# Two adapter layers in one kernel: another order of the engines' work within a step, and the gathers issued from GpSimd

## The chip, the cores and the metric

One NeuronCore of a Trainium2 chip runs the whole kernel. Its engines are TensorE (PE in the profile), VectorE (DVE), ScalarE (ACT), GpSimd (POOL) and SyncE (SP); each works through its own queue in order, and semaphores hold them together. DMAs are issued from SP's or GpSimd's queue and run on the core's 16 DMA engines. The metric is the time of one execution on the device, in microseconds (us); the time of a kernel is the median of its runs.

## What is computed

x is 64 sequences of 64 tokens with 1024 features, float32. There are two layers, each a LoRA adapter picked by sequence (rank 16), whose output goes through a dense 1024 x 1024 matrix with a bias and a mixture of four experts of rank 8, added to x.

```python
def cond(x, A, B, ids):                     # adapter of each sequence
    Bx = einsum('bni,bri->bnr', x, B[ids])
    return einsum('bnr,bor->bno', Bx, A[ids])

def ffn(c, W, b, EA, EB, RW, bias):         # layer 0: bias = Rb + log(prior)
    gates = softmax(c @ RW.T + bias)        # over 4 experts
    z = einsum('bth,erh->bter', c, EA)
    return c @ W.T + b + 2 * einsum('bter,eor,bte->bto', z, EB, gates)

x = x + ffn(cond(x, A0, B0, id0), W0, b0, ...)
x = x + ffn(cond(x, A1, B1, id1), W1, b1, ...)
```

## The kernel before

**Tiling.** x is kept with features on the partitions. The 64 sequences are cut into 8 steps of 8 sequences (512 tokens). Since the adapters have rank 16, a group of 8 adapters is 128 columns; the kernel never forms the adapters' output in full width but multiplies the adapters' A matrices with the weights (`wide`, 128 x 1060 per step) and then with the tokens' 128 coefficients. Every float32 operand is split into a high and a low part (ScalarE copies the high one, VectorE or GpSimd subtracts to get the low one), and each product is three matmuls (lines 307 to 309): high by high, low by high, high by low.

**A step on each engine** (`body(g, par, last)`; steps 1 to 6 run in a hardware loop on PE, ACT, DVE and POOL, see `steps`):
- SP: reads the 16 adapter ids of step g + 2 into registers (`pick`, L240), waits until step g + 1's adapters are all split (`a_lo`), issues 16 gathers (`gather`, L251 and L253: 64 KB into `b0raw` and 128 KB into `abraw` per sequence), and then stores the four chunks of the step's result from `xraw` (L282), each as soon as VectorE has written it (`d_out`), and loads the chunks of x of step g + 2 into the same buffer (L234), each when its chunk is stored.
- PE: the `ps_h` product (8 rounds over `hr`), `wide(0)`, the transposes of `hsb`, `route(0)`, `wide(1)`, half of `wide(2)`, the `ht` product, `turn()` (transposes `lp`, waits for softmax(0) by `l_done`), the rest of `wide(2)`, `query()` (waits for `htx_ready`, then for `l_lo` and `l_hi`), the first half of the next step's `project`, `route(1)`, the second half of `project`, `turn()`, and then the eight result tiles. A `wide` part has 8 rounds of three matmuls: parts 0 and 2 of 384 columns, part 1 of 292.
- ACT: high parts and PSUM reads in the order of PE's products: `split_b` (four copies into `bst_hi`), `wide_high(0)`, `ht` and `he`, two x copies (`split_x`, wait for the x loads by `x_in`), the exponential of softmax(0) (L686), `wide_high(1)`, `htx`, `coef_high(0)` (`ce_hi`, twice), the other x copies between `wide_high(2)` and the `cf` copies, and so on.
- DVE: low parts, softmax (L869 to L898), and the result tiles (L942: accumulator + bias + x).
- POOL: only the low parts of the first half of x (`xs_lo`, four pieces) and of the adapters' A (`a1s_lo`), L952. It issues DMAs only at the start of the kernel.

`b0raw` and `abraw` are single buffers, so the gather of step g + 2 can't start before step g + 1's adapters have been split. `xraw` is double, `xs` and `bst` are single. The last step holds back the last quarter of `wide(2)` until after the query.

## Time and profile before

| | us |
|---|---|
| median of 3 runs | 334.89 (334.20 to 335.64) |
| the profiled execution | 334.41 |
| its span in the trace | 332.70 |
| PE busy | 307.0 (92% of the span) |
| VectorE, ScalarE, GpSimd busy | 220.1, 186.4, 63.3 |

The span is the time between the first and the last event of the trace; the profiled execution took 1.71 us more than its span. PE's busy time counts overlapping matmuls once, and matmul ends are modelled, so pauses of PE are best read from the idle times that the trace puts ahead of an instruction, and from the distance of starts. The matmul clock granted was 1.00 of 2.4 GHz in the steps, 0.995 on average.

### The profile page before, as it was taken

The numbers are of one execution on the slowest core, as the hardware profiler recorded it, in microseconds if no ns is written. First come the engines' busy times: TensorE is split into PE (matmuls) and PEld (weight loads), VectorE is DVE, ScalarE is ACT, GpSimd is POOL, SyncE is SP. The second block draws the span as 40 slices with busy tenths as digits, with TensorE's granted clock in tenths as the row PEclk, the third lists the DMA queues.
The fourth block names the chain that finished last, engine by engine and source line by source line (L and its number), as shares of the span: only waits on it lengthen the run. The fifth ranks groups of instructions, "written<-read, shape, count | busy, mean of one in ns | idle before, by whom it ended". The sixth has DMA issues, their size and how long they took to land.

```text
span 332.7 us, 6476 instructions
## 1 busy us (share of the span) xinstructions
PE 307.0 (92%) x2048; PEld 284.4 (85%) x2048; DVE 220.1 (66%) x476; ACT 186.4 (56%) x384; POOL 63.3 (19%) x58
## 2 busy tenths in 40 slices
PE   5994998799989998999979999999999999999894
PEld 4453998589978998999979999999999999899783
DVE  2156887686738766686658666777668676864556
ACT  1446976946546565755466465646575657461520
POOL 5600000620042103320143003320332024200000
PEclk9999899999999999999999999999999999999999
DMA  7999973006870388126840587037811783041006
GB/s 267 345 365 381 347 208 156 0 8 167 300 224 0 104 243 302 51 60 212 286 139 0 158 284 250 2 103 244 299 47 55 255 292 92 0 193 62 1 0 252
DMA packets 30773, 56.16 MB, mean 169 GB/s; under 512 B 3633, under 2 KB 20050, under 8 KB 30754
## 3 DMA queue, kind: packets, MB, share of 16 engines
q1 hardware_dynamic: 29666, 52.97, 48.3%
q0 software_dynamic: 1088, 2.97, 2.5%
q8 instruction: 8, 0.13, 0.1%
q14 instruction: 11, 0.09, 0.1%
HBM read 39.15 MB, written 16.78 MB: 168 GB/s over the span
## 4 chain that ended last, share of the span: by engine, by line
issue 41%; PE 20%; DMA 13%; POOL 12%; DVE 6%; ACT 3%; SPq 2%; POOLq 1%; DVEq 0%; ACTq 0%
POOL xs_lo L952 8%; DMA out<-xraw 6%; DMA xraw<-x_in 6%; PE ps_d L307 3%; PE ps_d L309 3%; PE ps_d L308 3%; POOL a1s_lo L952 2%; DVE xs_lo L740 2%; DVE xraw L942 2%; PE ps_d L545 1%; PE ps_p L307 1%; PE ps_d L547 1%; ACT res L574 1%; SPq L253 1%; SPq L251 1%
## 5 line engine op out<-in xcount | busy, mean ns | idle before, releaser
L952 POOL TENSOR_TENSOR xs_lo<-xraw,xs_hi 128x512 fp32r<-128x512 f32 x28 | 36.0, 1290 | 182.5 <-ACT xs_hi L574 182.4
L307 PE MATMUL ps_d<-w1s_hi,a1s_hi 128*128 128x384 f32 (+1 forms) x192 | 63.9, 333 | 0.0
L309 PE MATMUL ps_d<-w1s_hi,a1s_lo 128*128 128x384 f32 (+1 forms) x192 | 62.0, 323 | 0.0
L308 PE MATMUL ps_d<-w1s_lo,a1s_hi 128*128 128x384 f32 (+1 forms) x192 | 61.9, 322 | 0.0
L942 DVE SCALAR_TENSOR_TENSOR xraw<-ps_d,lp,xraw 128x512 f32<-128x512 f32 x60 | 43.6, 748 | 22.5 <-PE ps_d L547 22.5
L574 ACT ACTIVATE xs_hi<-xraw 128x512 fp32r<-128x512 f32 x60 | 36.0, 626 | 26.4 <-DMA xraw<-x_in 25.9
L307 PE MATMUL ps_p<-xs_hi,bst_hi 128*128 128x256 f32 x120 | 36.5, 304 | 6.2 <-DVE bst_lo L740 2.4
L308 PEld LDWEIGHTS ps_d<-w1s_lo,a1s_hi 128*128 128x128 f32 x192 | 36.2, 189 | 0.0
L307 PEld LDWEIGHTS ps_d<-w1s_hi,a1s_hi 128*128 128x128 f32 x192 | 36.1, 188 | 0.0
L309 PEld LDWEIGHTS ps_d<-w1s_hi,a1s_lo 128*128 128x128 f32 x192 | 36.1, 188 | 0.0
L308 PE MATMUL ps_p<-xs_lo,bst_hi 128*128 128x256 f32 x120 | 34.5, 288 | 0.0
L309 PE MATMUL ps_p<-xs_hi,bst_lo 128*128 128x256 f32 x120 | 34.4, 287 | 0.0
L307 PE MATMUL ps_d<-cf,res 128*128 128x256 f32 x120 | 34.4, 286 | 0.0
L309 PE MATMUL ps_d<-cf,res 128*128 128x256 f32 x120 | 33.9, 282 | 0.0
L308 PE MATMUL ps_d<-cf,res 128*128 128x256 f32 x120 | 33.8, 281 | 0.0
L740 DVE TENSOR_TENSOR res<-ps_d,res 64x384 fp32r<-64x384 f32 (+1 forms) x48 | 24.3, 507 | 12.8 <-ACT res L574 12.3
L574 ACT ACTIVATE res<-ps_d 64x384 fp32r<-64x384 f32 (+1 forms) x48 | 21.3, 443 | 18.3 <-PE ps_d L309 17.9
L307 PEld LDWEIGHTS ps_p<-xs_hi,bst_hi 128*128 128x128 f32 x120 | 23.5, 196 | 9.4 <-DVE bst_lo L740 3.3
L952 POOL TENSOR_TENSOR a1s_lo<-abraw,a1s_hi 128x1024 fp32r<-128x1024 f32 x7 | 17.0, 2431 | 39.5 <-ACT a1s_hi L574 39.5
L545 PE MATMUL ps_d<-ce_hi,erows 128*128 128x512 f32 x60 | 24.3, 405 | 0.0
L308 PEld LDWEIGHTS ps_p<-xs_lo,bst_hi 128*128 128x128 f32 x120 | 23.6, 197 | 0.3
L547 PE MATMUL ps_d<-ce_lo,erows 128*128 128x512 f32 x60 | 23.7, 395 | 0.0
(227 smaller groups left out, 702.9 us busy)
## 6 DMA issues: line engine op xcount, KB each, us to landing
out<-xraw SPq DMA_DIRECT2D x31, 512.0 KB, 3.5
xraw<-x_in SPq DMA_DIRECT2D x28, 512.0 KB, 5.0
w_plain<-w SPq DMA_DIRECT2D x16, 512.0 KB, 8.9
abraw<-ab_tab SPq DMA_DIRECT2D x64, 128.0 KB, 2.1
b0raw<-b_tab SPq DMA_DIRECT2D x64, 64.0 KB, 2.0
xraw<-x_in POOLq DMA_DIRECT2D x4, 512.0 KB, 11.0
a_plain<-a SPq DMA_DIRECT2D x1, 512.0 KB, 3.6
out<-xraw SPq DMA_DIRECT2D x2, 256.0 KB, 2.7
```

Of the source, the lines that this page charges most:

```text
L251: sp.dma_start(b0raw[:, b, :], b0_tab[bass.ds(n0, 1)].rearrange("a p n -> p (a n)")).then_inc(signal, 16)
L253: sp.dma_start(abraw[:, b, :, :].rearrange("p a n -> p (a n)"), ab1_tab[bass.ds(n1, 1)].rearrange("a p n -> p (a n)")).then_inc(signal, 16)
L307: pe.matmul(acc, lh, rh, start=first, stop=False, skip_group_check=True)
L308: pe.matmul(acc, lh, rl, start=False, stop=False, skip_group_check=True)
L309: return pe.matmul(acc, ll, rh, start=False, stop=final, skip_group_check=True)
L545: pe.matmul(acc[:], erows[:, m * P:(m + 1) * P], ce_hi[:], start=False, stop=False, skip_group_check=True)
L547: pe.matmul(acc[:], erows[:, m * P:(m + 1) * P], ce_lo[:], start=False, stop=True, skip_group_check=True).then_inc(d_done, 1)
L574: return act.activation(dst, src, ACT.Copy)
L740: return dve.tensor_tensor(dst, whole, high.bitcast(F32), ALU.subtract)
L942: dve.scalar_tensor_tensor(out=xraw[par][:, m, :], in0=banks[m % len(banks)][:], scalar=bsum[:, m:m + 1], in1=xraw[par][:, m, :], op0=ALU. ...
L952: return pool.tensor_tensor(dst, whole, high.bitcast(F32), ALU.subtract)
```

## The change

Nothing is computed differently, and no computing instruction is added or removed; they are put in another order, and 112 gathers (of steps 1 to 7; those of step 0 stay on SP) move from SP's queue to GpSimd's. On SP, `pick` and `gather` leave `body`. On GpSimd, `gather(g + 2)` stands at the end of `body(g)`, behind `split_x` and `split_a`, and reads its 16 ids there, behind the wait on `a_lo`; that of step 1 stands ahead of the steps. GpSimd's loop now runs with its last three steps written out, as SP's did.

```diff
@@ block.sync
-            picks = pick(1)
-            sp.wait_ge(b_lo, 4)
-            sp.wait_ge(a_lo, 1)
-            gather(picks, range(GROUP))
...
-                if ahead:
-                    picks = pick(g + 2)
-                    sp.wait_ge(a_lo, g + 2)
-                    gather(picks, range(GROUP))
@@ block.tensor, body
-                    wide(0)
+                    wide(0, range(3))
...
                 route(0, f0x)
-                if not first:
-                    wide(1)
-                wide(2, range(KT // 2))
+                if first:
+                    wide(2, range(KT // 2))
+                else:
+                    wide(0, range(3, KT))
+                    wide(1, range(2))
                 pe.wait_ge(ht_lo, g + 1)
...
                 turn()
-                wide(2, range(KT // 2, 3 * KT // 4 if last else KT))
+                if first:
+                    wide(2, range(KT // 2, KT))
+                else:
+                    wide(1, range(2, KT))
...
                 query()
-                if last:
-                    wide(2, range(3 * KT // 4, KT))
+                if not first:
+                    wide(2)
...
-                    start_results((0, 1, 2, 3, 4))
+                    start_results((0, 1, 2, 3))
...
-                    from_layers(5)
-                    from_layers(6)
+                    for m in (4, 5, 6):
+                        from_layers(m)
@@ block.scalar, body (whole new order)
+                ht, he copies
+                softmax_exp(0)
+                if not last and not first:
+                    split_b(g + 1)
+                htx copies
+                coef_high(0)
+                wide_high(0)
+                if first:
+                    split_b(g + 1, QUARTERS[0:2])
+                if not last:
+                    split_x(g + 1, 1 - par, 0)
+                wide_high(1)
+                cf copies
+                if first:
+                    m0x_high(0, 2, ps_h)
+                wide_high(2)
+                if first:
+                    split_b(g + 1, QUARTERS[2:4])
+                if not last:
+                    split_x(g + 1, 1 - par, 1)
+                softmax_exp(1)
@@ block.vector, body (whole new order up to softmax(1))
+                c0_low(g); h_to_sbuf(g)
+                softmax(0)          # ht and he lows now inside it, ahead of the wait for exp_done
+                coef_low(0)
+                if not last:
+                    split_b(g + 1, (0, 1) if first else range(4))
+                wide_low(0)
+                the query's four pieces, cf lows
+                wide_low(1)
+                if first:
+                    split_b(g + 1, (2, 3))
+                split_second_x(g + 1, 1 - par, [0, 1, 2])
@@ block.gpsimd
+            def gather(g):
+                n0s, n1s = values(g * GROUP, GROUP, ADAPT0), values(g * GROUP + SEQS, GROUP, SEQS)
+                for b, (n0, n1) in enumerate(zip(n0s, n1s)):
+                    pool.dma_start(b0raw[:, b, :],
+                                   b0_tab[bass.ds(n0, 1)].rearrange("a p n -> p (a n)")).then_inc(gathered, 16)
+                    pool.dma_start(abraw[:, b, :, :].rearrange("p a n -> p (a n)"),
+                                   ab1_tab[bass.ds(n1, 1)].rearrange("a p n -> p (a n)")).then_inc(gathered, 16)
...
             def body(g, par, last):
                 if not last:
                     split_x(g + 1, 1 - par, 0, range(CH))
                     split_a(g + 1)
-
-            steps(pool, body)
+                if not (isinstance(g, int) and g >= STEPS - 2):
+                    pool.wait_ge(a_lo, g + 2)
+                    gather(g + 2)
+
+            pool.wait_ge(b_lo, 4)
+            pool.wait_ge(a_lo, 1)
+            gather(1)
+            steps(pool, body, 3)
```

For ACT and DVE the piece of the diff above tells the new order in short; a line there that isn't code names a group of copies.

**ScalarE, the part of a loop step from the `ht` copy to the softmax's exponential.** `lg<-lg` is the exponential. Before:

```order
L574 ACTIVATE ht<-ps_t 128x128 [waits ht_done]
L574 ACTIVATE he<-ps_t 32x128
L579 REGISTER_ALU
L580 ISA [waits x_in0]
L574 ACTIVATE xs_hi<-xraw 128x512 [waits x_used]
L580 REGISTER_ALU [waits x_in1]
L574 ACTIVATE xs_hi<-xraw 128x512 [waits x_used]
L685 ISA
L686 ACTIVATE lg<-lg 128x16 [waits sm_step]
```

and now, up to the coefficients (`ce_hi`):

```order
L571 ACTIVATE ht<-ps_t 128x128 [waits ht_done]
L571 ACTIVATE he<-ps_t 32x128
L678 ISA
L679 ACTIVATE lg<-lg 128x16 [waits sm_step]
L583 REGISTER_ALU
L571 ACTIVATE bst_hi<-abraw 128x4x8x16 [waits gathered]
L571 ACTIVATE bst_hi<-b0raw 128x4x8x16 x2
L571 ACTIVATE bst_hi<-abraw 128x4x8x16
L571 ACTIVATE htx<-ps_h 64x256 [waits htx_done]
L571 ACTIVATE htx<-ps_h 64x256
L672 ISA
L571 ACTIVATE ce_hi<-ps_t 64x512 [waits t_done]
```

The two x copies with their waits for `x_in` have left the place ahead of the exponential, and the four copies from the gathered buffers, which stood at the step's start, are now between the exponential and `htx`.

**GpSimd, the end of a loop step.** Before:

```order
L952 TENSOR_TENSOR xs_lo<-xraw,xs_hi 128x512 [waits x_hi]
L956 REGISTER_ALU
L952 TENSOR_TENSOR xs_lo<-xraw,xs_hi 128x512 [waits x_hi]
L962 REGISTER_ALU
L952 TENSOR_TENSOR a1s_lo<-abraw,a1s_hi 128x8x8x16 [waits a_hi]
L956 ISA
L952 TENSOR_TENSOR xs_lo<-xraw,xs_hi 128x512 [waits x_hi]
```

and now:

```order
L941 TENSOR_TENSOR xs_lo<-xraw,xs_hi 128x512 [waits x_hi]
L951 REGISTER_ALU
L941 TENSOR_TENSOR a1s_lo<-abraw,a1s_hi 128x8x8x16 [waits a_hi]
L978 ISA [waits a_lo]
L978 TENSOR_LOAD ids
L978 ISA x17
L978 TENSOR_LOAD ids
L978 ISA x16
L985 ISA
L985 DMA b0raw<-b_tab 128x128
L987 ISA
L987 DMA abraw<-ab_tab 128x256
```

Behind `a1s_lo` the next step's first `xs_lo` followed; now two loads of eight ids and 16 DMAs (the last two rows repeat eight times) stand between.

**PE, from the `ht` product of a loop step to the next `wide` rounds.** Before:

```order
L309 MATMUL ps_d<-w1s_hi,a1s_lo 128x384
L478 MATMUL ps_h<-ht,pick 128x128 [waits ht_lo]
L478 MATMUL ps_h<-ht,pick 128x128
L481 REGISTER_ALU
L445 MATMUL ps_t<-ident,lp 128x128 [waits l_done]
L445 MATMUL ps_t<-ident,lp 128x128 x3
L307 MATMUL ps_d<-w1s_hi,a1s_hi 128x384
```

and now:

```order
L301 MATMUL ps_d<-w1s_hi,a1s_lo 128x292
L472 MATMUL ps_h<-ht,pick 128x128 [waits ht_lo]
L472 MATMUL ps_h<-ht,pick 128x128
L475 REGISTER_ALU
L437 MATMUL ps_t<-ident,lp 128x128 [waits l_done]
L437 MATMUL ps_t<-ident,lp 128x128 x3
L299 MATMUL ps_d<-w1s_hi,a1s_hi 128x292
```

The turn has moved forward in the step: it now stands in the middle of part 1 (292 columns) instead of part 2 (384), and all of part 2 comes after the query.

## Rows read from the trace of the kernel before

**Rows 1.** Busy time by stretch, steps 1 to 6; columns are named in the first line.

```profile
core 0: us, PE busy (x) PEld busy (x) DVE busy (x) ACT busy (x) POOL busy (x), PEclk, DMA share, GB/s
...
154.58:191.75 37.17, 35.13 (x248) 33.62 (x247) 24.79 (x56) 21.27 (x46) 7.56 (x5) 1.00 0.51 160
...
262.80:297.82 35.02, 34.81 (x249) 33.59 (x247) 25.37 (x56) 21.28 (x46) 7.62 (x5) 1.00 0.48 167
sum 216.49, PE 209.88 PEld 201.62 DVE 151.03 ACT 127.71 POOL 45.49; mean PE 34.98 PEld 33.60 DVE 25.17 ACT 21.29 POOL 7.58
```

**Rows 2.** The same view, step 0.

```profile
40.37:81.33 40.96, 37.20 (x256) 34.70 (x255) 30.81 (x62) 27.69 (x55) 7.51 (x5) 1.00 0.36 107
```

**Rows 3.** Waits of the whole span: who for whom, us in all, times, longest.

```profile
ACT xs_hi L574 <- DMA xraw<-x_in: 25.9, 18, 2.6
...
PE ps_t L445 <- DVE lp L898: 6.2, 6, 1.7
```

**Rows 4.** Timeline, SP's queue: start, us, instruction.

```profile
155.38 0.96 SPq L282 DMA_DIRECT2D out<-xraw  x2
158.83 0.35 SPq L234 DMA_DIRECT2D xraw<-x_in  x1
```

**Rows 5.** Timeline, ScalarE; in brackets the idle time ahead and its releaser.

```profile
166.92 0.63 ACT L574 ACTIVATE xs_hi<-xraw 128x512 fp32r<-128x512 f32 x1 [2.62 <-DMA xraw<-x_in]
```

**Rows 6.** Timeline, PE, the turn of the same step.

```profile
169.30 0.66 PE L445 MATMUL ps_t<-ident,lp 128*128 128x128 f32 x4 [1.73 <-DVE lp L898]
```

**Rows 7.** Timeline, PE, in the fastest step (from 262.80).

```profile
276.72 0.34 PE L307 MATMUL ps_d<-w1s_hi,a1s_hi 128*128 128x384 f32 x1
277.25 0.34 PE L307 MATMUL ps_d<-w1s_hi,a1s_hi 128*128 128x384 f32 x1
...
279.02 0.40 PE L494 MATMUL ps_s<-ce_hi,he 128*128 128x512 f32 x1
...
285.91 0.39 PE L307 MATMUL ps_p<-xs_hi,bst_hi 128*128 128x256 f32 x1
```

**Rows 8.** Timeline, ScalarE, in the same step.

```profile
265.13 0.63 ACT L574 ACTIVATE bst_hi<-abraw 128x512 fp32r<-128x512 f32 x1 [0.49 <-PE ps_h L316]
...
266.71 0.62 ACT L574 ACTIVATE bst_hi<-abraw 128x512 fp32r<-128x512 f32 x1
...
275.83 0.78 ACT L574 ACTIVATE htx<-ps_h 64x256 fp32r<-64x256 f32 x2 [0.97 <-PE ps_h L478]
...
277.13 0.63 ACT L574 ACTIVATE ce_hi<-ce_hi 64x512 fp32r<-64x512 f32 x1
```

**Rows 9.** Timeline, GpSimd, in step 0 and in step 6.

```profile
58.50 5.08 POOL L952 TENSOR_TENSOR xs_lo<-xraw,xs_hi 128x512 fp32r<-128x512 f32 x4 [44.59 <-ACT xs_hi L574]
...
286.53 2.43 POOL L952 TENSOR_TENSOR a1s_lo<-abraw,a1s_hi 128x1024 fp32r<-128x1024 f32 x1 [5.37 <-ACT a1s_hi L574]
```

**Rows 10.** Line 240, SP's reading of ids: ns min/median/max, first and last start.

```profile
L240 SPq SEQ_ASSERT  x128: 18/18/33, 6.6 to 245.2; - x128
L240 SPq TENSOR_LOAD <-ids x16: 522/527/741, 5.6 to 242.7; - x16
```

**Rows 11.** Tile `exp_plain`, four dynamic DMAs from GpSimd's queue: same columns.

```profile
L971 POOLq MOVE exp_plain<-exp x4: 29/29/29, 3.7 to 5.6; - x4
L971 POOL DMA_DIRECT2D exp_plain<-exp x4: 537/537/547, 4.3 to 6.1; - x4
...
DMA to landing us min/median/max: 5.3/5.5/5.7
```

**Rows 12.** DMA issues: queue, count, KB each, median us from issue to landing.

```profile
abraw<-ab_tab SPq DMA_DIRECT2D x64, 128.0 KB, 2.1
...
ident<-identity POOLq DMA_DIRECT2D x1, 64.0 KB, 3.8
```

**Rows 13.** Timeline, VectorE, the `cf` pieces of step 0 and of step 6.

```profile
62.89 1.41 DVE L740 TENSOR_TENSOR cf<-cm,cf 64x256 fp32r<-64x256 f32 x2 [2.34 <-ACT cf L574]
...
281.65 0.87 DVE L740 TENSOR_TENSOR cf<-cm,cf 64x256 fp32r<-64x256 f32 x2 [0.16 <-ACT cf L574]
```

**Rows 14.** Timeline, PE, route(1) of the last step.

```profile
316.78 0.27 PE L314 MATMUL ps_z<-f1s,cf 128*128 128x72 f32 x1 [2.07 <-DVE cf L740]
```

More of the change, by code:

```diff
@@ L245, in pick, with gather @@
                 return tuple(zip(values(g * GROUP, GROUP, ADAPT0), values(g * GROUP + SEQS, GROUP, SEQS)))
-            def gather(picks, seqs, signal=gathered):
+            def gather(picks, seqs, signal):
                 for b in seqs:
@@ L663, in body @@
                 first = isinstance(g, int) and g == 0
-                if not last and not first:
-                    act.wait_ge(h_done, g + 1)
-                    split_b(g + 1)
                 def wide_high(n):
@@ L686, in softmax_exp @@
                     act.activation(ex[:], lg[:], ACT.Exp).then_inc(exp_done, 1)
-                wide_high(0)
                 act.wait_ge(ht_done, g + 1)
@@ L691, in body @@
                 copy(he[0:LR, :], ps_t[0:LR, P:2 * P]).then_inc(ht_hi, 1)
+                softmax_exp(0)
                 if not last and not first:
-                    split_x(g + 1, 1 - par, 0, [0, 1])
-                softmax_exp(0)
-                wide_high(1)
+                    split_b(g + 1)
                 act.wait_ge(htx_done, g + 1)
@@ L703, in body @@
                 if not last:
-                    split_x(g + 1, 1 - par, 0, range(CH) if first else [2, 3])
-                wide_high(2)
-                if first:
-                    split_b(g + 1, QUARTERS[2:4])
-                if not last:
-                    split_x(g + 1, 1 - par, 1, [0])
+                    split_x(g + 1, 1 - par, 0)
+                wide_high(1)
                 act.wait_ge(c1_done, 2 * g + 1)
@@ L717, in body @@
                     m0x_high(0, 2, ps_h)
+                wide_high(2)
+                if first:
+                    split_b(g + 1, QUARTERS[2:4])
                 if not last:
-                    split_x(g + 1, 1 - par, 1, range(1, CH))
+                    split_x(g + 1, 1 - par, 1)
                 softmax_exp(1)
@@ L845, in body @@
                     h_to_sbuf(g)
-                if not last and not first:
-                    split_b(g + 1)
                 def wide_low(n):
@@ L883, in softmax @@
                                       ALU.subtract).then_inc(sm_step, 1)
+                    if layer == 0:
+                        dve.wait_ge(ht_hi, 2 * g + 2)
+                        low(ht[:, 1, :], ps_t[:, 0:P], ht[:, 0, :])
+                        low(he[ELO, :], ps_t[0:LR, P:2 * P], he[0:LR, :]).then_inc(ht_lo, 1)
                     if layer == 1 and not last:
@@ L900, in softmax @@
                                       .to_broadcast([P, TT, EXP, ER]), ALU.mult).then_inc(l_done, 1)
+                softmax(0)
+                coef_low(0)
+                if not last:
+                    split_b(g + 1, (0, 1) if first else range(4))
                 wide_low(0)
-                dve.wait_ge(ht_hi, 2 * g + 2)
-                low(ht[:, 1, :], ps_t[:, 0:P], ht[:, 0, :])
-                low(he[ELO, :], ps_t[0:LR, P:2 * P], he[0:LR, :]).then_inc(ht_lo, 1)
-                softmax(0)
-                wide_low(1)
-                coef_low(0)
-                if first:
-                    split_b(g + 1, (0, 1))
                 dve.wait_ge(q_done, g + 1)
@@ L985, in _, with values @@
                                ).then_inc(x0_in[i], 16)
+            def values(first, count, limit):
+                return nc.values_load_multi_w_load_instructions(
+                    ids[0:1, bass.ds(first, count)], (mybir.EngineType.Pool,), min_val=0, max_val=limit - 1)[1]
+            def gather(g):
[5 more added lines that the diff above has]
+                                   ab1_tab[bass.ds(n1, 1)].rearrange("a p n -> p (a n)")).then_inc(gathered, 16)
             def body(g, par, last):
```

## The prediction

> **What bounds the kernel now.** I read the stretches by step first, then the list of waits, then single rows. A step here runs from PE's first matmul of one `body` (the `ps_h` product) to that of the next. The six steps 1 to 6 take 216.49 us together, PE is busy for 209.88 of it at granted clock 1.00 (2.4 GHz), and one step takes between 35.0 and 37.2 us [rows 1]; step 0 takes 40.96 us [rows 2]. So the matmuls set the time and little can be won: only PE's pauses. In the list of waits one is large: PE's `turn()` waits six times for `lp`, 6.2 us in all [rows 3]. The cause lies upstream. ScalarE waits 25.9 us in 18 places for `xraw<-x_in` [rows 3], and in a loop step the second of these waits stands ahead of the exponential of softmax(0): it cost 2.62 us at 166.92 [rows 5], and PE's turn, which needs that softmax, waited 1.73 us [rows 6]. The x blocks are late because SP issues 16 gathers first; its first store of the step goes out at 155.38 and its first x load at 158.83 [rows 4], 0.8 us and 4.3 us after the step began at 154.58, though the first result tiles had been finished during the tail of the step before.
>
> **What goes.** (a) SP without gathers stores and loads about 6 us earlier, so ScalarE no longer waits for x. (b) ScalarE also does the exponential before any x copy. (c) On PE, between route(0) and the turn there stand 15 matmuls of 384 columns and 6 of 292 instead of 24 and 12; that is shorter (about 3.4 us), but softmax(0) now has VectorE to itself and needs about 2.7 us. So I cost the turn's wait at nothing; its cover is 0.7 us. The fastest step, 262.80 to 297.82, is the one without that wait, 35.02 us [rows 1]. Two pauses remain in it: one of 0.30 us ahead of the matmul at 285.91 [rows 7] and a like one some 2.5 us earlier, both behind VectorE's late `xs_lo` pieces. With a punctual gather they shrink to nearly nothing, so an unhindered step is 34.6 us, and six are 207.6: **-8.9 us**. (d) In the last step PE waits 2.07 us for `cf` ahead of route(1) [rows 14]; six matmuls were its cover (part 2, the last quarter), and now 24 are, 4.2 us. The wait goes: **-2.2 us** with its restart. (e) Step 0: its turn no longer waits, up to 0.9 us, but Pool's pieces end when they did, so PE only waits later. VectorE, already late there (its two `cf` pieces took 1.41 instead of 0.87 us, since it stood behind Pool's `xs_lo` until 63.58) [rows 9, 13], now has the four lows of part 1 ahead of the `b` and second `x` pieces. Bounds: -0.9 to one Pool piece more, 5.08 / 4 = +1.3 [rows 9]; I take **+1.0**, near the upper end, because PE waits for VectorE at that place now.
>
> **What comes: the gather is late.** Pool's `a1s_lo` ends at 288.96 [rows 9], 8.9 us before the next step begins at 297.82. From here on in step time (0 is that beginning): SP had its ids in registers when this came; Pool reads them after the wait. On SP the last load of eight begins at 242.7 and its last assertion at 245.2 [rows 10]: 2.5 us for eight, 5.0 for 16, and Pool is at -3.9. Then 16 DMAs. Four dynamic ones on Pool had their address moves from 3.7 to 5.6, one per 0.6 us, each starting 0.6 us after its move [rows 11]. So the sixteenth starts at -3.9 + 0.6 + 15 x 0.6 = +5.7. On SP the same sixteen were out at about 0. When do they land? SP's gathers took 2.1 us and Pool's first DMA, with few transfers before it, 3.8 us [rows 12]; Pool's `exp_plain` with all 16 engines busy took 5.3 to 5.7 [rows 11]. Bounds 2.1 and 5.5; I take 3.8, the row nearest to the case: the gather now runs beside the stores and x loads, of which one or two are in flight. **Landing at +9.5.**
>
> Who waits: ScalarE's `split_b`, whose place moved from the step's start to behind the exponential (+6.3: h product 2.0, nine matmuls 1.6, transposes and route(0) 1.3 until VectorE has them, its four pieces 1.1, the exponential 0.3), and everything behind it: `htx`, `ce_hi`, then PE's query. Four copies take 2.2 us (265.13 to 267.33), then from the start of `htx` to the end of the second `ce_hi` it is 1.9 us (275.83 to 277.76) [rows 8], and VectorE's `ce_lo` ends with it: query's second half can start at 9.5 + 2.2 + 2.0 + 0.1 = +13.8. PE reaches it earlier than now: before, at 279.02 - 262.80 = 16.2; without the eight rounds of part 2, 0.53 us each (276.72 to 277.25), at +12.0 [rows 7]. **Wait: 1.8 us per step** (0.1 with SP's landing of 2.1, 3.5 with 5.5). Part 2 behind the query doesn't hide it, since PE works in order.
>
> Second, what followed in time on an engine is now pressed together: VectorE does the four `bst_lo` and two `cf` pieces while Pool does `xs_lo`. In step 0 a `cf` piece stood until Pool was done [rows 9, 13]. Late ScalarE copies put Pool's 5.1 us just ahead of the first half's product and route(1). On time there is 1.3 us of room, late there is none. Bounds 0 and 1.3 us (one Pool piece); I take **0.5**. The Trainium skill says the same, in SBUF — State Buffer, section Who interferes with whom: a DVE instruction with two SBUF inputs contends with a GpSimd one that reads SBUF, the second blocks. By that rule, the trace agrees (1.41 against 0.87 us) [rows 13].
>
> **Sum.** -8.9 - 2.2 + 1.0 = -10.1 us, and 6 x (1.8 + 0.5) = +13.8 us: +3.7. The profiled execution took 334.41 us (its span of 332.70 and 1.71 around it), so 338.1; the median of the runs is 0.48 above it: **338.6 us**. The gather counts six times, since the gathers of steps 2 to 7 are issued at the end of steps 0 to 5; that of step 1 may start at 35.5 us, when `a1s_lo` of step 0 is done, so it lands at about 35.5 + 5.0 + 0.6 + 9.0 + 3.8 = 54, ahead of step 0's first `b` copy (by the rows of before not earlier than 56).
>
> **Rivals.**
> 1. **The gather is on time.** Landing as fast as SP's, 2.1 us, gives +7.8, the wait is 0.1 and Pool's pieces find room: 334.9 - 10.1 + 0.6 = 325 us. For it: one step's traffic is 5.6 MB for 35 us, DMA share 0.48 to 0.51 [rows 1], so the engines aren't full on average. Against it: no DMA of Pool in this trace landed in less than 3.8 us, and stores, loads and gathers now fall in the same 15 us. Chance 0.15. The Trainium skill, DMA: Bandwidth & Descriptors, section on the anatomy of one DMA (SWDGE), gives 2.0 us plus bytes by 436 GB/s, for 128 KB 2.3 us; as an estimate by that page the wait is 0.3 us and the time about 326. The trace doesn't agree where it can be seen (3.8 us for 64 KB).
> 2. **Half late.** Landing after about 3 us: +8.7, wait 1.0, press 0.2: 334.9 - 10.1 + 7.2 = 332 us. Chance 0.13.
> 3. **Even.** After about 3.4 us the wait is 1.4 and the press 0.3, which gives back just what was won: 335 us. Chance 0.15.
> 4. **The forecast**, slower. The tipping point between faster and slower is a loss of 1.7 us per step (10.1 / 6), a landing at about +9.1. Chance 0.42.
> 5. **Much later.** With x loads in all engines Pool's DMAs land after 5 us: wait 3.0, press 0.7, 334.9 - 10.1 + 22.2 = 347 us. Chance 0.15.
>
> **How the numbers follow.** Likeliest is case 4, 338.6 us. The range goes down to 327 and up to 348: case 1 is left out below for the most part (0.13) and the far part of case 5 above (0.06). About 0.5% (1.7 us) is what a measurement of this kernel can tell from no change. Faster: cases 1 and 2, 0.28. Same: 0.15. Slower: 0.57. The likeliest case's own range is 336.6 to 343.
>
> **What would show it.** Right: ScalarE's first `bst_hi` of a loop step has an idle time ahead of it released by the DMA of `abraw` or `b0raw`, some 3 us in steps 1 to 6, and PE idles 1.5 to 2.5 us at `ps_s` (query), no longer at the turn; Pool's first gather DMA starts some 5.6 us after `a1s_lo` ends and the last 9 us later; route(1) of the last step starts without a wait; SP's first store of a step comes some 6 us before the step's begin. Wrong in the sense of case 1: no idle time ahead of `bst_hi` and steps of 34.6 us. What else would break it: ids read faster on Pool than on SP, a pitch of its DMAs below 0.5 us (then everything is 1.5 us earlier and the kernel is faster), or x copies that still wait for DMA because loads and gathers share the engines.

## The result

The changed kernel takes **363.87 us** (median of 4 runs, 361.95 to 365.15); the kernel before, run beside it on the same chip, 335.26 us. The ratio is 1.0856, interval 1.0811 to 1.0901. The prediction was 338.6 us with a range of 327 to 348.

The stretches of the changed kernel by step (same view and columns as [rows 1, 2]; the first row is step 0, then three of the six loop steps with the sum of all six, then the last step):

```profile
core 0: us, PE busy (x) PEld busy (x) DVE busy (x) ACT busy (x) POOL busy (x), PEclk, DMA share, GB/s
40.52:84.48 43.96, 39.65 (x256) 37.50 (x255) 31.41 (x62) 28.11 (x55) 20.03 (x28) 0.92 0.36 117
...
124.78:165.92 41.14, 36.84 (x249) 35.64 (x247) 25.68 (x56) 21.46 (x46) 16.83 (x22) 0.92 0.41 142
...
289.60:330.84 41.24, 36.51 (x249) 34.78 (x247) 25.69 (x56) 21.45 (x46) 14.32 (x17) 0.96 0.38 142
sum 246.36, PE 220.31 PEld 211.74 DVE 154.12 ACT 128.72 POOL 97.25; mean PE 36.72 PEld 35.29 DVE 25.69 ACT 21.45 POOL 16.21
...
330.84:363.40 32.56, 27.70 (x190) 26.37 (x188) 18.71 (x45) 9.43 (x23) 0.00 (x0) 0.96 0.21 84
```

The six loop steps went from 216.49 [rows 1] to 246.36 us, 29.9 more; step 0 from 40.96 [rows 2] to 43.96, 3.0 more; the last step from 34.88 to 32.56, 2.3 less. With 0.15 us at the start that is the 30.7 us between the spans 332.7 and 363.4.

Who waits (columns as [rows 3]). ScalarE no longer waits for x, but for the gather, once in each loop step:

```profile
POOL b0raw L985 <- issue: 62.5, 10, 27.8
...
ACT bst_hi L571 <- DMA abraw<-ab_tab: 38.0, 6, 6.8
...
ACT xs_hi L571 <- DMA xraw<-x_in: 3.0, 3, 1.4
...
PE ps_t L437 <- DVE lp L890: 0.3, 1, 0.3
```

The wait for x, 25.9 us before [rows 3], is down to these 3.0, all of them in the first 25 us, and that of the turn is down from 6.2 to 0.3: in the steps both are gone, as forecast. One round of the new wait follows, from the timelines (start, us, instruction, idle time ahead and its releaser), in order of time. ScalarE, the step from 165.92:

```profile
178.66 0.63 ACT L571 ACTIVATE bst_hi<-abraw 128x512 fp32r<-128x512 f32 x1 [6.54 <-DMA abraw<-ab_tab]
...
180.87 0.78 ACT L571 ACTIVATE htx<-ps_h 64x256 fp32r<-64x256 f32 x2
```

PE in the same step, the last matmul of part 1 and the query that waits for `htx`:

```profile
177.02 0.29 PE L301 MATMUL ps_d<-w1s_hi,a1s_lo 128*128 128x292 f32 x1
181.71 0.58 PE L299 MATMUL ps_s<-cf,htx 128*128 128x256 f32 x1 [4.39 <-ACT htx L571]
```

VectorE, from the coefficients' low part on; up to `lg` at 194.41, which ScalarE's exponential waits for, it has no idle time:

```profile
182.17 0.68 DVE L731 TENSOR_TENSOR ce_lo<-ps_t,ce_hi 64x512 fp32r<-64x512 f32 x1 [8.83 <-ACT ce_hi L571]
```

ScalarE, later in the step:

```profile
194.63 0.22 ACT L679 ACTIVATE lg<-lg 128x16 f32<-128x16 f32 x1 [1.51 <-DVE lg L869]
194.75 1.04 ACT L571 ACTIVATE a1s_hi<-abraw 128x1024 fp32r<-128x1024 f32 x1
```

GpSimd, from there on (14 more DMAs at the same pitch up to the last row):

```profile
195.87 2.43 POOL L941 TENSOR_TENSOR a1s_lo<-abraw,a1s_hi 128x1024 fp32r<-128x1024 f32 x1 [5.53 <-ACT a1s_hi L571]
203.99 0.55 POOL L985 DMA_DIRECT2D b0raw<-b_tab  x1 [5.69 <-issue]
204.59 0.54 POOL L987 DMA_DIRECT2D abraw<-ab_tab  x1
...
212.75 0.54 POOL L987 DMA_DIRECT2D abraw<-ab_tab  x1
```

ScalarE, in the next step:

```profile
220.14 0.63 ACT L571 ACTIVATE bst_hi<-abraw 128x512 fp32r<-128x512 f32 x1 [6.78 <-DMA abraw<-ab_tab]
...
222.35 0.78 ACT L571 ACTIVATE htx<-ps_h 64x256 fp32r<-64x256 f32 x2
```

These rows close a **loop**. From `htx` to `a1s_hi` 13.88 us, to `a1s_lo` 1.12, to the first gather DMA 8.12 (the subtraction's 2.43 and the 5.69 in which GpSimd reads 16 ids), to the sixteenth DMA 8.76 (one per 0.58), to the first copy of what has landed 7.39, to the next `htx` 2.21: together 41.48 us, the distance of the two `htx` (222.35 - 180.87) and the step's length. That the pieces add up to that distance is only arithmetic. What makes them a loop is that each begins when the one before lets it: `htx` stands right behind the copies of B, VectorE works through its row without a gap, `a1s_hi` follows the exponential, `a1s_lo` follows `a1s_hi`, the ids and the DMAs follow `a1s_lo`, and the copies of B wait for the DMAs. No piece waits for PE. So it is not a step of 35 us with a wait on top; the gather calls itself again, and a microsecond taken out of the loop should shorten the step by as much, until something else is longer. The experiments try that.

Of the DMAs the page says (queue, count, KB, median us from issue to landing), beside 2.1 and 2.0 on SP before [rows 12]:

```profile
xraw<-x_in SPq DMA_DIRECT2D x28, 512.0 KB, 6.6
...
abraw<-ab_tab POOLq DMA_DIRECT2D x56, 128.0 KB, 6.5
b0raw<-b_tab POOLq DMA_DIRECT2D x56, 64.0 KB, 6.4
```

The DMA engines are full just then. Over the step from 165.92 their mean share is 0.42, but from the start of its gather's sixteenth DMA (171.51) to the copy (178.66) it is 0.98:

```profile
171.51:178.66 7.15, 5.80 (x42) 5.57 (x40) 1.64 (x8) 0.22 (x1) 0.54 (x1) 1.00 0.98 366
```

After PE's pause the granted clock is at half: 0.50 of 2.4 GHz from 181.7 to 186, and 1.00 again from 187 on; the matmul at 181.71 takes 0.58 us. The stretches show it as 0.92 in the first four loop steps and 0.96 in the last two.

### The profile page after: what moved, and what is told of

Read it like the earlier page. It is cut to its first block, busy times and chain, and to the rows that moved or that the text cites. A ratio compares the mean times of both kernels' runs of the same rounds, so it can differ in the third digit from the quotient of the medians.

```text
span 363.4 us, 6464 instructions
## 1 busy us (share of the span) xinstructions
PE 319.7 (88%) x2048; PEld 297.1 (82%) x2048; DVE 223.5 (62%) x476; ACT 187.8 (52%) x384; POOL 127.6 (35%) x171
## 4 chain that ended last, share of the span: by engine, by line
issue 22%; DVE 19%; PE 17%; DMA 15%; ACT 10%; POOLq 8%; POOL 7%; DVEq 0%; ACTq 0%
DMA abraw<-ab_tab 11%; POOLq L978 6%; DVE bst_lo L731 4%; POOL a1s_lo L941 4%; ACT bst_hi L571 4%; DVE xs_lo L731 4%; DMA xraw<-x_in 3%; PE ps_d L299 3%; PE ps_d L300 3%; PE ps_d L301 3%; DVE res L731 2%; ACT a1s_hi L571 2%; DVE ps_s L904 2%; DVE cm L907 1%; DVE xraw L931 1%
## 5 line engine op out<-in xcount | busy, mean ns | idle before, releaser
L941 POOL TENSOR_TENSOR xs_lo<-xraw,xs_hi 128x512 fp32r<-128x512 f32 x28 | 40.0, 1458 | 81.4 <-ACT xs_hi L571 81.4
L299 PE MATMUL ps_d<-w1s_hi,a1s_hi 128*128 128x384 f32 (+1 forms) x192 | 66.7, 348 | 0.0
L300 PE MATMUL ps_d<-w1s_lo,a1s_hi 128*128 128x384 f32 (+1 forms) x192 | 64.6, 337 | 0.0
L301 PE MATMUL ps_d<-w1s_hi,a1s_lo 128*128 128x384 f32 (+1 forms) x192 | 64.5, 336 | 0.0
L985 POOL DMA_DIRECT2D b0raw<-b_tab x56 | 30.2, 539 | 64.5 <-issue 62.5
L731 DVE TENSOR_TENSOR ce_lo<-ps_t,ce_hi 64x512 fp32r<-64x512 f32 x16 | 10.9, 683 | 61.5 <-ACT ce_hi L571 61.5
L299 PEld LDWEIGHTS ps_d<-w1s_hi,a1s_hi 128*128 128x128 f32 x192 | 38.9, 203 | 0.6
L301 PE MATMUL ps_p<-xs_hi,bst_lo 128*128 128x256 f32 x120 | 35.4, 295 | 0.0
L987 POOL DMA_DIRECT2D abraw<-ab_tab x56 | 30.1, 538 | 3.7 <-issue 1.3
L571 ACT ACTIVATE bst_hi<-abraw 128x512 fp32r<-128x512 f32 x16 | 9.9, 620 | 38.1 <-DMA abraw<-ab_tab 38.0
L299 PE MATMUL ps_s<-cf,htx 128*128 128x256 f32 x16 | 6.4, 402 | 25.2 <-ACT htx L571 25.2
```

What stands on the lines that cost most here:

```text
L299: pe.matmul(acc, lh, rh, start=first, stop=False, skip_group_check=True)
L300: pe.matmul(acc, lh, rl, start=False, stop=False, skip_group_check=True)
L301: return pe.matmul(acc, ll, rh, start=False, stop=final, skip_group_check=True)
L571: return act.activation(dst, src, ACT.Copy)
L731: return dve.tensor_tensor(dst, whole, high.bitcast(F32), ALU.subtract)
L941: return pool.tensor_tensor(dst, whole, high.bitcast(F32), ALU.subtract)
```

## The experiments

Each kernel ran beside the kernel before on the same chip; ratios are against that.

### Which half of the change costs

`e_order`: the new order of all engines, the gathers on SP as before.

```diff
+                if ahead:
+                    picks = pick(g + 2)
+                    sp.wait_ge(a_lo, g + 2)
+                    gather(picks, range(GROUP))
...
-                if not (isinstance(g, int) and g >= STEPS - 2):
-                    pool.wait_ge(a_lo, g + 2)
-                    gather(g + 2)
```

> The new order of PE, ACT and DVE alone; all gathers stay on SP's queue as in the kernel before, ids read ahead of the wait. Theory (the late gather of GpSimd's queue is the loss, and with it the halved clock): ScalarE's first bst_hi of a loop step has no wait for a gather, PE none at ps_s, granted clock 1.00; SP's stores and x loads are late again, but ScalarE now wants x only at about +12 us of a step, so some 1 us of waits is left: steps of 35 to 36 us, 326 to 333 us in all. Rival (the order itself loses, since VectorE and GpSimd are pressed together and ScalarE reads PSUM later): steps of 38 us or more, over 345 us.

Measured: 338.84 us, ratio 1.0142 (1.009 to 1.0193). That lies between my two ranges. The order alone doesn't win 10 us, it loses 4. Its stretches, two of the loop steps with the sum of all six, and step 0:

```profile
157.70:195.52 37.82, 36.27 (x248) 34.99 (x247) 24.06 (x56) 21.35 (x46) 8.10 (x5) 0.95 0.51 159
195.52:231.48 35.96, 34.96 (x249) 33.56 (x247) 24.08 (x56) 21.38 (x46) 8.07 (x5) 1.00 0.50 158
...
sum 218.88, PE 212.41 PEld 204.21 DVE 144.51 ACT 128.22 POOL 48.53; mean PE 35.40 PEld 34.03 DVE 24.09 ACT 21.37 POOL 8.09
```

```profile
40.48:84.42 43.94, 39.66 (x256) 37.51 (x255) 31.37 (x62) 28.05 (x55) 7.61 (x5) 0.92 0.36 108
```

So of the 29.9 us in the loop steps 2.4 are the order's (218.88 - 216.49) and 27.5 the gather's (246.36 - 218.88), 4.6 a step; step 0's 3.0 us are there without the late gather. These are differences of single profiled executions: `before` and `e_last` below have the same code in these six steps, and their sums differ by 1.2 us (216.49 and 215.33), so 2.4 is not much. No step comes near the 34.6 that I had put down: at full clock they take 35.7 to 36.1, two have a stretch of half clock and take some 1.8 more.

`e_queue`: the old order, the gathers on GpSimd.

```diff
-                if ahead:
-                    picks = pick(g + 2)
-                    sp.wait_ge(a_lo, g + 2)
-                    gather(picks, range(GROUP))
...
+                if not (isinstance(g, int) and g >= STEPS - 2):
+                    pool.wait_ge(a_lo, g + 2)
+                    gather(g + 2)
```

> The old order of all engines; only the gathers of steps 1 to 7 are issued from GpSimd's queue, behind split_a, ids read there. Theory: the gather lands at about +12.7 us of a step as in the changed kernel (363.9 us); in the old order split_b stands at the step's start, so ht, the exponential and the turn wait for it too: PE pauses 5 to 6 us per step and the clock falls: 365 to 380 us. Rival (the gather is harmless and the order is the loss): under 340 us.

Measured: 387.93 us, ratio 1.1613 (1.1528 to 1.1698), above what I expected. Its steps take 44.4 to 45.4 us. B is split here ahead of everything else in the step; I take it that the same loop is longer by that, but have not summed it. Its row of the waits:

```profile
ACT bst_hi L566 <- DMA abraw<-ab_tab: 64.9, 6, 11.0
```

So the loss doesn't need the new order: with the old one the late gather costs more (a wait of 64.9 instead of 38.0 us).

### Taking time out of the loop

`e_ids_ahead`: the changed kernel, but GpSimd reads the 16 ids at the start of its body, ahead of its other work.

```diff
             def body(g, par, last):
+                if ahead:
+                    picks = pick(g + 2)
...
                     pool.wait_ge(a_lo, g + 2)
-                    gather(g + 2)
+                    gather(*picks)
```

> The changed kernel, but GpSimd reads the 16 ids of step g + 2 at the start of body(g), ahead of the x pieces, when it has nothing to do, and not behind the wait on a_lo. Theory (serial time on the gather's path, 5.6 us ids and first issue, 8.8 us for 16 issues, 6.6 us landing): it lands 5 us earlier, at about +7.7, PE's pause at ps_s goes or is under 0.5 us, granted clock 1.00, steps of 34.6 to 35.5 us: 325 to 331 us. Rival (the landing is bound by the x traffic on the DMA engines, not by the issue): it lands hardly earlier, over 345 us.

Measured: 337.94 us, ratio 1.0137 (1.0061 to 1.0213): 26 us of the 29 are gone, though not all that I expected. One round of the loop here:

```profile
128.34 0.78 ACT L571 ACTIVATE htx<-ps_h 64x256 fp32r<-64x256 f32 x2
...
146.46 0.55 POOL L988 DMA_DIRECT2D b0raw<-b_tab  x1 [0.67 <-POOL a1s_lo L941]
...
155.27 0.54 POOL L990 DMA_DIRECT2D abraw<-ab_tab  x1
...
162.35 0.63 ACT L571 ACTIVATE bst_hi<-abraw 128x512 fp32r<-128x512 f32 x1 [1.49 <-DMA abraw<-ab_tab]
...
164.57 0.79 ACT L571 ACTIVATE htx<-ps_h 64x256 fp32r<-64x256 f32 x2
```

Behind `a1s_lo` 0.67 us are left of the 5.69, so the reading itself was 5.0 us. From `htx` to the first gather DMA it is now 18.12 us instead of 23.12, to the sixteenth 8.81, to the copy 7.08, to the next `htx` 2.22: 36.23 us. The loop still sets the steps: 5.0 us were taken from it, and the steps fell by 4.4 in the mean, to 36.6 (sum 219.83). Its mark is that ScalarE still waits for the gather once in each loop step, 11.5 us in all. The median landing is 4.8 us.

`e_small_x`: the changed kernel, but in the loop SP stores and loads only the first eighth of each block of x, so most of the result is left out.

```diff
+                    n = TOK if last else TOK // 8
-                                 xraw[par][:, KC * i:KC * (i + 1), :]).then_inc(stored[i], 16)
+                                 xraw[par][:, KC * i:KC * (i + 1), 0:n]).then_inc(stored[i], 16)
```

> The changed kernel with the x loads of steps 2 to 7 and the stores of steps 0 to 6 cut to an eighth of the tokens (64 of 512), so that the DMA engines carry almost only the gathers; the rest of x is old data and most of the output isn't written. Theory (contention with 512 KB transfers makes the 6.6 us from issue to landing): median landing of the gathers falls to 2.3 to 3.8 us, PE's pause at ps_s to 1 to 2 us, 336 to 346 us. Rival (GpSimd's descriptors are slow by themselves): landing stays over 5.5 us and the time over 355 us.

Measured: 338.29 us, ratio 1.0113 (1.0052 to 1.0174). The gathers come from the same queue at the same place; the page's DMA issues (columns as above):

```profile
abraw<-ab_tab POOLq DMA_DIRECT2D x56, 128.0 KB, 2.5
b0raw<-b_tab POOLq DMA_DIRECT2D x56, 64.0 KB, 2.5
```

They land in 2.5 instead of 6.5 us. The 4 us are the traffic of x beside them, not GpSimd's queue. The loop is still there (ScalarE waits for the gather in all six loop steps, 13.0 us), with 2.3 to 2.9 us in place of the 7.39 from the sixteenth DMA to the copy. By the sum above this leaves 36.4 to 37.0 us, and the steps take 36.4 to 37.8 (the 37.8 is one whose sixteen DMAs took 10.0 us instead of 8.8).

`e_fill`: the changed kernel with 19 matmuls of no use where PE pauses.

```diff
+                if not first and not last:
+                    for _ in range(19):
+                        pe.matmul(ps_z[:], erows[:, 0:P], erows[:, 0:TOK], start=True, stop=True,
+                                  skip_group_check=True)
                 query()
```

> The changed kernel with 19 more matmuls of 512 columns ahead of the query of steps 1 to 6. They read weights that are there since the start and write a PSUM bank that nobody reads at that time, so they add about 4.1 us of work that stands where TensorE now waits 3.4 to 4.6 us for the gather; they change nothing of the result. Theory (a part of the loss is the halved clock after the pause, since matmuls of the step run at 0.58 instead of 0.28 us until 4.6 us of work are done): the clock stays at full speed in steps 1 to 6, the pause itself stays as long as the gather is late, and each of the four steps with 0.92 gives back about 2.3 us, each of the two with 0.96 about 1.7 us: 364 - 12.6 = 351 us, between 348 and 355. Rival (the clock costs nothing, since the gather of the next step sets the pace anyway): within 2 us of 364. Second rival (the added matmuls are late work of their own): 366 to 372.

Measured: 365.29 us, ratio 1.0876 (1.0801 to 1.0951), as the changed kernel. The first rival holds, my theory falls. The clock stayed up and the steps stayed long; two of its loop steps, and ScalarE in the first of them:

```profile
166.12:206.71 40.59, 39.77 (x267) 37.24 (x266) 25.68 (x56) 21.37 (x46) 16.79 (x22) 1.00 0.42 141
206.71:247.98 41.27, 40.02 (x268) 37.15 (x266) 25.70 (x56) 21.37 (x46) 16.83 (x22) 1.00 0.41 142
```

```profile
180.41 0.78 ACT L575 ACTIVATE htx<-ps_h 64x256 fp32r<-64x256 f32 x2
...
194.29 1.04 ACT L575 ACTIVATE a1s_hi<-abraw 128x1024 fp32r<-128x1024 f32 x1
```

From `htx` to `a1s_hi` it is again 13.88 us, now with PE at full clock. The half clock costs nothing in the loop: VectorE's row sets that stretch, and it has no gap in either kernel. A busy PE (39.8 of 40.6 us, with matmuls of no use among them) is no sign that it bounds.

### What holds a step of the new order

In `e_order` ScalarE still waits for x (22.9 us, [rows 3] had 25.9), and VectorE for `cf` behind it; its waits:

```profile
ACT xs_hi L579 <- DMA xraw<-x_in: 22.9, 15, 2.4
...
DVE cf L739 <- ACT cf L579: 17.5, 7, 3.9
```

`v_woven`: SP issues half of the gathers, and the rest between the stores and loads of x.

```diff
-                    gather(picks, range(GROUP))
+                    gather(picks, range(0, 4))
...
+                    if ahead and i == 1:
+                        gather(picks, range(4, 6))
+                    if ahead and i == 2:
+                        gather(picks, range(6, 8))
```

> The new order of the engines, all gathers by SyncE's queue, but woven among the stores and loads of x: the first four sequences, store 0, two sequences, store 1 and load 0, the last two sequences, and so on. What tells it from the new order with the gathers in one piece (338.8 us) is that loads of x leave some 2 to 4 us sooner. If late loads of x are what holds that kernel (the copy to xs_hi waits 22.9 us in sum for them, the sum cf behind it comes late, and two steps lose 1.8 us to a halved clock): 334 to 336 us. If the projection is bound by the low parts of x on GpSimd and VectorE whatever the loads do, as the kernel with early ids (36.0 to 36.2 us a step, no wait for x) has it: 337 to 339.

Measured: 335.92 us, ratio 1.0021 (0.9978 to 1.0065), at the edge of the first range. The wait for x falls from 22.9 to 9.7 us, but the loop steps only from 218.88 to 218.51. Where x is on time, the gather is late again: its last DMA leaves SP's queue 3.4 to 4.3 us after the beginning of the step and not at about the beginning, and ScalarE waits 0.9 to 2.2 us for it in the first five loop steps. It doesn't in the sixth, and that one is the shortest of all:

```profile
ACT bst_hi L583 <- DMA abraw<-ab_tab: 8.0, 5, 2.1
...
265.17:300.04 34.87, 34.61 (x248) 33.47 (x247) 25.69 (x56) 21.52 (x46) 8.24 (x5) 1.00 0.41 144
```

Step 0 is 42.81 us here with the clock at 1.00, 1.1 less than in `e_order`, but PE began it 1.8 us sooner (38.72 against 40.48) and came to the turn later in the step. From the turn on like stands against like: 54.23 to 84.42 in `e_order`, 30.19 us, and 53.01 to 81.53 here, 28.52, with the same waits for the low parts of x. So of step 0's 3.0 us the half clock is 1.7, and 1.3 are left for the order.

`v_both`: the same, with step 0 of ScalarE and VectorE in the old order.

```diff
+                if first:
+                    wide_high(0)
                 act.wait_ge(ht_done, g + 1)
...
-                wide_high(0)
+                if not first:
+                    wide_high(0)
```

> The one before it, with step 0 of ScalarE and VectorE back in the old order; steps 1 to 7 keep the new. Step 0 took 43.9 us in the new order and 40.96 in the old; if the order alone does that, this kernel is 3 us under the woven one (331 to 333 if that has 335). If step 0 is long for another reason (the gathers of step 1), within 1 us of it.

Measured: 334.79 us, ratio 1.0013 (0.9973 to 1.0054). Step 0 is 40.95 us again, so the order does it, not the gathers of step 1: ahead of the first b pieces stand the evictions of part 0. The medians differ by 1.1 us, near the 1.3 above and not the 3 that I expected. The loop steps, whose code is the woven kernel's, came out 1.7 us longer in the profiled run (220.20); that much such a sum varies. Their lengths follow the wait for the gather: 35.4 and 35.8 us where it is 0.7 and 0.8, 36.9 to 37.6 where it is 1.9 to 2.8.

What PE waits for in the loop of `v_both` is small and spread: 0.5 us for `f1s`, 0.25 to 0.45 for `xs_lo` of either engine, a few tenths between the projection's matmuls. The timeline of VectorE in `e_ids_ahead`, from the coefficients' low part on:

```profile
129.64 0.68 DVE L731 TENSOR_TENSOR ce_lo<-ps_t,ce_hi 64x512 fp32r<-64x512 f32 x1 [3.57 <-ACT ce_hi L571]
130.25 0.68 DVE L731 TENSOR_TENSOR bst_lo<-abraw,bst_hi 128x512 fp32r<-128x512 f32 x1
...
135.54 2.57 DVE L731 TENSOR_TENSOR cf<-cm,cf 64x256 fp32r<-64x256 f32 x2
138.14 0.19 DVE L731 TENSOR_TENSOR f1s<-ps_d,f1s 64x36 fp32r<-64x36 f32 x1
...
139.26 1.90 DVE L731 TENSOR_TENSOR xs_lo<-xraw,xs_hi 128x512 fp32r<-128x512 f32 x3
```

It stands 3.57 us ahead of `ce_lo` and then works for 13 us without a gap, which makes this row a link of the loop in `e_ids_ahead` and in the changed kernel. The four `bst_lo`, which the old order had at the step's start, and the lows of parts 0 and 1, which it had ahead of `ce_lo`, are now inside, and two `cf` take 2.57 instead of 0.87 us [rows 13] beside GpSimd's `xs_lo`.

`v_both2`: ScalarE copies x ahead of the evictions of part 0, VectorE subtracts part 0 behind `cf`.

```diff
                 else:
+                    wide_high(0)
                     wide_high(1)
...
                 if not first:
+                    wide_low(0)
                     wide_low(1)
```

> The one before it, and in steps 1 to 6 two more moves: ScalarE copies the four chunks of x for GpSimd ahead of its evictions of the first wide product (1.0 us), and VectorE subtracts that product's low part (1.13 us) behind the sum cf instead of ahead of it. If the projection waits for the low parts of x because they start too late, its waits of 0.4 to 1 us a step go and the kernel is 3 to 6 us under the one before (326 to 330). If what holds it is the pace of GpSimd's and VectorE's subtractions (1.45 and 0.62 us a chunk, each slower while the other runs), within 1 us of it.

Measured: 345.17 us, ratio 1.0284 (1.0197 to 1.0371), 10 us worse, which neither of my ranges had. The moved subtraction went ahead of `f1s`, and PE now waits 0.9 to 2.1 us for it in a loop step, with half clock behind it. ScalarE's move is in the same run; half of it stands alone in the next one.

`v_x_early`: instead of that, ScalarE copies only the first two chunks of x ahead of part 0's evictions.

```diff
+                if not first and not last:
+                    split_x(g + 1, 1 - par, 0, [0, 1])
                 if not first:
                     wide_high(0)
```

> The woven kernel with step 0 in the old order (334.8 us), and one move: in steps 1 to 6 ScalarE copies the first two chunks of x ahead of its evictions of the first wide product instead of behind them, so GpSimd starts its low parts 1.0 us sooner; VectorE's order stays. Theory (each step over 35.0 us is long because the projection waits for low parts of x that are started too late: 0.4 for GpSimd's, 0.4 for VectorE's, some smaller ones, 0.8 to 1 us in the gaps of the projection's matmuls): 0.4 to 0.9 us a step go, 329.5 to 332.5 us. Rival (VectorE's f1s and cf come as late as before or later, as in the kernel with two moves, where they cost 1 to 2 us a step): 335 to 340.

Measured: 334.32 us, ratio 1.0 (0.9971 to 1.003); loop steps 219.37, again between my ranges. GpSimd starts 1 us sooner after `htx` and it doesn't matter: its start isn't what holds the steps.

`v_b_first`: `v_both`, and VectorE does the four `bst_lo` in the wait ahead of `ce_lo`.

```diff
+                if not last and not first:
+                    split_b(g + 1, range(4))
                 coef_low(0)
-                if not last:
-                    split_b(g + 1, (0, 1) if first else range(4))
+                if first:
+                    split_b(g + 1, (0, 1))
```

> The woven kernel with step 0 in the old order (334.8 us, steps 1 to 6 at 36.7 in the mean), and one move on VectorE in steps 1 to 6: it subtracts the four low parts of B ahead of the coefficients' low part ce_lo instead of behind it. There VectorE waits 2.4 to 3.5 us for ScalarE's ce_hi, and the high parts of B are 0.6 to 2.4 us old by then; from ce_lo to the turn of the second layer it works without a gap (204.0 to 217.3 us). Theory (VectorE is what bounds that stretch, and the projection's waits for f1s, 0.5, for xs_lo, 0.25 to 0.45, and the small ones in its gaps come from there): everything behind ce_lo is 1.8 to 2.4 us sooner, the waits go, steps 1 to 6 take 35.2 to 35.9, and the kernel 328 to 331 us. Rival (GpSimd's subtractions or the loads of x set the projection's pace): within 1 us of 334.8. Second rival (ce_lo comes late, since the fourth quarter of B is copied only when ce_hi is due, and TensorE waits for it): slower, 336 to 338.

Measured: 332.02 us, ratio 0.9876 (0.9802 to 0.995): faster than the kernel before, though 1 us above the range that I expected. The loop steps fell to 216.59 us in all, from 220.20 in `v_both` and 218.51 in `v_woven`, which have one loop code; the sum row of its stretches:

```profile
sum 216.59, PE 211.12 PEld 201.68 DVE 151.19 ACT 128.44 POOL 45.40; mean PE 35.19 PEld 33.61 DVE 25.20 ACT 21.41 POOL 7.57
```

So VectorE's row held the woven kernels back, by 0.3 to 0.6 us a step; behind it comes ScalarE at once, whose copies of x and `cf` stand one behind another. The sum is just that of the kernel before (216.49): what this kernel has over it is the last step. VectorE's timeline, the wait that is left:

```profile
209.25 1.10 DVE L752 TENSOR_TENSOR cf<-cm,cf 64x256 fp32r<-64x256 f32 x2 [2.90 <-ACT cf L583]
```

I had expected steps of 35.2 to 35.9 us; they take 36.1 in the mean, the last three of them 35.2 to 35.8.

`v_b_first_whole`: the same with the gathers in one piece on SP, as in `e_order`.

```diff
-                    gather(picks, range(0, 4))
+                    gather(picks, range(GROUP))
...
-                    if ahead and i == 1:
-                        gather(picks, range(4, 6))
-                    if ahead and i == 2:
-                        gather(picks, range(6, 8))
```

> The same with the gathers of a step in one piece on SyncE's queue, as the kernel before has them, so that B is there when ScalarE wants it (the woven gathers come 0.9 to 2.8 us late in some steps) but the loads of x are 2 to 4 us later. If VectorE is the bound and the late gathers are what is left: 1 to 2 us under the woven one (327 to 329). If the loads of x, over xs_hi and the sum cf behind it, then end the stretch (as 2.62 us of wait for cf in the new order alone): 332 to 336, the gain of the move is lost.

Measured: 336.57 us, ratio 1.0063 (1.0019 to 1.0107). The gain is lost again, as the second theory says: VectorE's wait for `cf` is 30.4 us in all, against 14.8 in the woven one. The loop steps are 219.89 us, no less than `e_order`'s 218.88. Where x is late, VectorE has idle time in its row anyway, and neither of the two moves helps without the other.

### The last step

`e_last`: the kernel before, with the new order in its last step only.

```diff
-                    wide(0)
+                    wide(0, range(3) if last else range(KT))
...
-                    wide(2, range(3 * KT // 4, KT))
+                    wide(2)
```

> The kernel before with the new order in its last step alone (no step after it hangs on that order). The last step took 35.2 us before and 32.6 in every kernel with the new order, since the 2.07 us in which TensorE waited for the sum cf are gone. If that is the order's own doing: 2.2 to 2.6 us under the kernel before beside it, ratio 0.993. If the last step owes it to what the steps ahead of it leave (loads and copies done earlier): within 0.5 us of the kernel before.

Measured: 331.64 us, ratio 0.9933 (0.9905 to 0.9962), 2.3 us under the kernel before beside it. The last step, in the stretches:

```profile
296.51:329.00 32.49, 27.68 (x190) 26.35 (x188) 18.72 (x45) 9.43 (x23) 0.00 (x0) 0.97 0.21 85
```

It takes 32.5 us, as in every kernel with the new order. This is the one part of the change that pays by itself.

## Why the prediction was wrong

The direction was right (slower, 0.57) and for the reason given: the gather is late and PE waits for it at the query. The size was 3.7 us where the spans show 30.7, and 25 of the 27 missing microseconds are in the six loop steps (+4.9 forecast, +29.9 measured). Step by step:

- **The wait, 1.8 + 0.5 us a step, +13.8**: this is the step that failed. The difference to the kernel with SP's gathers is 4.6 us a step, 27.5 in all. Even with the landing put right, the form of the sum was wrong. I took the time at which the gather is issued as fixed to the step's beginning and added the wait once; but the issue hangs on `a1s_lo`, that on the same step's `htx`, and that on the gather. The loop has to be summed as a loop, 41.48 us, and then it is the step's length: what the step would be otherwise, my 34.6 us, drops out. With my own 3.8 us of landing and the other pieces as measured it would have given 41.5 - 2.7 = 38.8 us a step, and so some 348 us.
- **Landing after 3.8 us, at +9.5**: it landed after 6.5 in the median, and ScalarE's copy began at 178.66, +12.7. The value and its upper bound of 5.5 were both too low: I wrote that the gather runs beside the stores and x loads, and then took the row of a DMA that ran with little beside it. `e_small_x` (2.5 us without that traffic) shows that the traffic makes the difference. Rival 1 argued from a mean DMA share of 0.48 to 0.51 that the engines aren't full; in the stretch that counts they are, 0.98. The Trainium skill's fit (DMA: Bandwidth & Descriptors, anatomy of one DMA) gives, as an estimate, 2.3 us for 128 KB. The 2.5 us of `e_small_x` agree with it; among the x blocks, at 6.5 us, it doesn't hold.
- **The gather's place, ids 5.0 us, last DMA at +5.7**: 5.69 us with the first issue in it, 5.0 without, and at 171.51 the last one started, +5.6. Right. The pitch was 0.58 where I had 0.6.
- **VectorE pressed beside GpSimd, 0.5 us**: two `cf` in 2.55 to 2.57 us in the changed kernel and in `e_ids_ahead`, 0.87 in [rows 13]. Seen as predicted, but it is 1.7 us, above my bound of 1.3, and since VectorE's row is a link of the loop it is a part of the 13.88 us there.
- **"An unhindered step is 34.6 us, -8.9"**: no kernel here has six such steps. With SP's gathers the new order takes +2.4 us on the six (`e_order`), 11.3 us from my term, but there x is late; woven, the gather is late. In the one loop step in which neither cost more than 0.34 us, the last of `v_woven`, it took 34.87 us. So the value was nearly right and the condition was not: I took for granted that nothing new would be late. I also looked for PE's old pauses instead of adding up VectorE's work from `ce_lo` on, where the four `bst_lo` and the lows of parts 0 and 1 went. `v_b_first` shows 1.9 to 3.6 us of it, in the woven kernels only. (a) came true: the changed kernel's first store of a step comes 6.2 us before the step, at 159.73. It bought nothing, since the loop set the step.
- **The last step, -2.2 us**: -2.3 measured, and `e_last` gives it alone. Right, with its cause.
- **Step 0, +1.0 us**: +3.0. Place and cause are right (VectorE and the evictions ahead of the b pieces, shown by `v_both`). The order's part is 1.3, at my upper bound; the other 1.7 are a stretch of half clock behind the waits, which the prediction didn't count.
- **The rivals**: the fifth (landing after 5 us, 347) had the nearest place and a chance of only 0.15. That the clock would fall was in none; it fell, and it cost nothing in the loop steps of the changed kernel.

What stays open: of the 35.7 to 36.1 us of a step of `e_order` at full clock the shares of VectorE, of ScalarE, and of x and the gather landing late are not told apart. No run has both on time in all steps, and none moves the four `bst_lo` in `e_ids_ahead`, where by the sum it would shorten the loop.

## What to carry to other kernels

When a transfer's issue waits for work that itself needs the transfer before it, add up the whole round and compare it with the step: if it is longer, it is the step's length, and neither PE's share nor its clock counts. The test is to take a known time out of one link and see whether the step falls by as much. When work is moved out of an engine's wait, look at what stands ahead of it and behind it on the engine where it goes; here, with x on time, four subtractions were cheap in front of `ce_lo` and dear behind it. And a landing time is that of the traffic beside it: for a transfer that is moved into the stores and loads, take the row of one that ran among them, and the DMA share of that stretch, not of the step.

## What the runs showed of the hardware

The same dynamic DMA of 128 KB from GpSimd's queue lands in 2.5 us with little traffic (`e_small_x`), in 4.8 us when issued 5 us earlier (`e_ids_ahead`), and in 6.5 us in the midst of the x blocks. The mean share of the DMA engines in those steps is only 0.38 to 0.42; from the start of the sixteenth DMA to the copy it is 0.98. Getting from `a1s_lo` to the first DMA took GpSimd 5.69 us with 16 ids to read and 0.67 us without. A dynamic DMA took it 0.58, and SP 0.51.

The granted clock fell to half after pauses of 3.4 to 4.6 us in the changed kernel, where it cost nothing; with 19 filler matmuls in the pause it stayed at 1.00. It fell also in two steps of `e_order` whose pauses in the projection were each under 0.8 us. In step 0 it fell in `e_order`, and behind the same pauses (2.04 and 0.96 us the longest) it stayed at 1.00 in `e_ids_ahead` and `v_woven`; that stretch of half clock cost `e_order` 1.7 us.
